# Odd experts' weighted sum moved from VectorE to ScalarE and GpSimd in a decoder layer's mixture of experts

## The reference

```python
logits = jnp.einsum('bsd,de->bse', input, Wg)
probs = jax.nn.softmax(logits, axis=-1)
top_vals, top_idx = jax.lax.top_k(probs, TOP_K)          # E = 8, TOP_K = 2
top_vals = top_vals / jnp.sum(top_vals, axis=-1, keepdims=True)
onehot = jax.nn.one_hot(top_idx, E, dtype=input.dtype)
mask = jnp.sum(onehot, axis=2)
scores = jnp.sum(onehot * top_vals[..., None], axis=2)
xm = input[None] * jnp.moveaxis(mask, -1, 0)[..., None]
h = jax.nn.relu(jnp.einsum('ebsd,edh->ebsh', xm, W1) + b1[:, None, None, :])
y = jnp.einsum('ebsh,ehd->ebsd', h, W2) + b2[:, None, None, :]
out = jnp.sum(y * jnp.moveaxis(scores, -1, 0)[..., None], axis=0)
```

## Time and profile before

| What | Value |
|---|---|
| Runs (median of three) | 512.89 us |
| Profiled execution, first to last instruction (its span) | 510.6 us |
| Mean granted TensorE clock | 0.843 |
| TensorE matmuls busy | 401.5 us (79%) |
| VectorE busy | 323.2 us (63%) |
| ScalarE busy | 159.2 us (31%) |
| GpSimd busy | 39.3 us (8%) |
| VectorE weighted adds, L1410 | 128 instructions, 36.0 us |

### The profile page before, as it was taken

How to read it: one execution, slowest core, us unless ns; L and a number is a source line. 1 busy time by engine, 2 the same in 40 slices (tenths; PEclk the granted TensorE clock), 3 DMA queues, 4 the chain that set the end, 5 groups by cost and what they waited for, 6 DMA issues and landing times.

```text
span 510.6 us, 8321 instructions
## 1 busy us (share of the span) xinstructions
PE 401.5 (79%) x2952; PEld 293.4 (57%) x2952; DVE 323.2 (63%) x1050; ACT 159.2 (31%) x267; POOL 39.3 (8%) x77
## 2 busy tenths in 40 slices
PE   1979999788973699984245689897998979887992
PEld 0647677467962699971023355565656546564672
DVE  2043464677999823368763576676897588777635
ACT  1252523512345211142021124422433244413430
POOL 7000000002980000000000000000000000000000
PEclk9989999997997555575555969999899989999997
DMA  7460201039653900000000000000020000000000
GB/s 246 105 186 1 42 0 22 1 75 296 166 145 88 119 3 3 3 2 0 1 1 27 15 21 1 0 22 0 2 62 2 21 0 21 0 0 1 22 2 21
DMA packets 48305, 22.23 MB, mean 44 GB/s; under 512 B 17768, under 2 KB 47632, under 8 KB 48016
## 3 DMA queue, kind: packets, MB, share of 16 engines
q1 hardware_dynamic: 31760, 13.40, 10.9%
q10 hardware_dynamic: 16512, 8.39, 6.0%
HBM read 18.64 MB, written 3.15 MB: 43 GB/s over the span
## 4 chain that ended last, share of the span: by engine, by line
PE 49%; DVE 31%; issue 9%; DMA 5%; ACT 3%; SPq 2%; DVEq 0%; ACTq 0%; POOL 0%
PE bank L460 9%; PE bank L493 5%; PE bank L691 5%; PE bank L699 5%; PE bank L721 5%; PE bank L733 4%; PE bank L442 4%; DVE prod L1430 3%; DVE inv L1432 3%; DVE as_t L1410 2%; DVE as_t L1232 2%; DVE nt L1143 2%; DVE nt L1142 2%; DVE as_t L1223 2%; DVE sm L1144 2%
## 5 line engine op out<-in xcount | busy, mean ns | idle before, releaser
L699 PEld LDWEIGHTS bank<-w_sb,as_t 128*128 128x128 f32 x512 | 61.0, 194 | 23.0 <-issue 18.8
L699 PE MATMUL bank<-w_sb,as_t 128*128 128x128 f32 x512 | 63.9, 280 | 5.0 <-ACT as_t L1002 5.0
L1002 ACT ACTIVATE as_t<-bank,cb 128x512 f32<-128x512 f32 x64 | 43.4, 687 | 76.0 <-PE bank L691 60.8
L691 PE MATMUL bank<-as_t,w_sb 128*128 128x512 f32 x128 | 66.5, 648 | 0.0
L1410 DVE SCALAR_TENSOR_TENSOR as_t<-bank,as_t 128x128 f32<-128x128 f32 x128 | 36.0, 344 | 23.4 <-PE bank L699 21.1
L460 PE MATMUL bank<-wtap,xc_pad 128*128 128x384 f32 x128 | 47.0, 514 | 3.8 <-DVE wtap L1157 3.8
L721 PE MATMUL bank<-vb,early 32*32 32x32 f32 x512 | 29.9, 236 | 11.7 <-DMA early<-inverses 11.7
L442 PE MATMUL bank<-ident,as_t 128*128 128x128 f32 (+1 forms) x64 | 12.1, 319 | 33.8 <-DVE as_t L1232 15.7
L1201 DVE TENSOR_TENSOR as_t<-bank,masks 128x512 f32 (+1 forms) x32 | 21.3, 690 | 26.7 <-PE bank L493 26.7
L460 PEld LDWEIGHTS bank<-wtap,xc_pad 128*128 128x128 f32 x128 | 25.0, 202 | 20.3 <-issue 4.3
L721 PEld LDWEIGHTS bank<-vb,early 32*32 32x32 f32 x512 | 28.2, 151 | 13.1 <-issue 12.3
(11 more groups left out here) (221 smaller groups left out, 647.5 us busy)
## 6 DMA issues: line engine op xcount, KB each, us to landing
toep<-taps_long ACTq DMA_DIRECT2D x8, 1024.0 KB, 7.0
toep<-x SPq DMA_DIRECT2D x8, 256.0 KB, 2.8
early<-x SPq DMA_DIRECT2D x4, 256.0 KB, 4.6
w_sb<-w SPq DMA_DIRECT2D x1, 1024.0 KB
w_sb<-w SPq DMA_DIRECT2D x2, 512.0 KB
blocks<-as_t SPq DMA_DIRECT2D x16, 64.0 KB, 2.0
early<-blocks SPq DMA_DIRECT2D x1, 1024.0 KB, 4.9
toep<-ctx_in SPq DMA_DIRECT2D x4, 256.0 KB, 3.4
```

What stands on the lines that cost most here:

```text
L691: pe.matmul(ps[4 + half][:, :], w1_sb[:, e, half * 128:half * 128 + 128], x2_c.rearrange("p b t -> p (b t)"), start=True, stop=True).then_ ...
L699: last = pe.matmul(bank(6 + e % 2)[:, b, :], hid[:, e % 2, half, b * L:(b + 1) * L], w2_sb[:, e, half, :], start=(half == 0), stop=(half = ...
L1002: act.activation(hid[:, e % 2, half, :], ps[4 + half][:, :], ACT.Relu, bias=c_of("b1", 2 * e + half)).then_inc(s["hid_ready"], 1)
```

## The change

The even experts' results (bank 6) are still summed on VectorE into acc. The odd experts' results (bank 7) are taken out of PSUM by ScalarE, which multiplies each sequence's 128 columns by its score (four activations of 128 x 128): expert 1 straight into a new tile `acc_odd`, experts 3, 5 and 7 into two alternating tiles `y_odd`. GpSimd adds these three to `acc_odd`, one 128 x 512 tensor_tensor each. `finish` on VectorE first adds `acc_odd` to acc. Each bank has its own counter: `y_added` now counts even experts and `y_scaled` odd ones. In all, VectorE loses 64 of its 128 weighted adds and gains 4 additions of 128 x 512, ScalarE gains 64 activations and GpSimd 12 additions.

```diff
--- before.py
+++ after.py
@@ -201,6 +201,8 @@
         hid = over(2 * 2 * N).rearrange("p (s k n) -> p s k n", s=2, k=2)
         acc = over3(G, D)
         fin = over3(G, D)
+        acc_odd = over3(G, D)
+        y_odd = over(2 * G * D).rearrange("p (k b c) -> p k b c", k=2, b=G)
         ps = [stack.enter_context(nc.psum_tensor(f"bank{i}", [128, 512], F32)) for i in range(8)]
@@ -242,7 +244,7 @@
                  "att_ps x2_ready "
                  "x2t_ps x2c_ready route_ps rmax_ready rexp_ready score_ready scoret_ps scoret_ready binit_ps hid_ps "
-                 "hid_ready y_ps sum_started y_added fin_ready").split()
+                 "hid_ready y_ps sum_started y_added y_scaled odd_added fin_ready").split()
         s = {n: sem(n) for n in names}
@@ -250,10 +252,10 @@
         CREDITS = {
             "pe": {"proj_ready": 1, "q_ps": 1, "kh_ps": 1, "kb_ps": 1, "gram_ps": 1,
                    "z_ps": 1, "st_ps": 1, "st2_ps": 1, "y_ps": 2},
-            "act": {"kb_c": 2, "proj_free": 2, "onc_ready": 1, "hid_ready": 2},
-            "dve": {"vb_ready": 1, "gram_kept": H, "x1_ready": 1, "x2_ready": 1, "ostats_ready": 1, "y_added": 2,
+            "act": {"kb_c": 2, "proj_free": 2, "onc_ready": 1, "hid_ready": 2, "y_scaled": 1},
+            "dve": {"vb_ready": 1, "gram_kept": H, "x1_ready": 1, "x2_ready": 1, "ostats_ready": 1, "y_added": 1,
                     "fin_ready": 1, "sum_started": 1},
-            "pool": {"v_kept": 1},
+            "pool": {"v_kept": 1, "odd_added": 1},
         }
         credit = {n: k for of in CREDITS.values() for n, k in of.items()}
@@ -429,8 +431,21 @@
             pool.wait_ge(s["stats_ready"], 4)
             stats_of(0)
             pool.wait_ge(s["stats_ready"], 5)
-            with pool.Fori(1, NG) as g:
-                stats_of(g)
+            stats_of(1)
+
+            def add_odd(g):
+
+                for e in (3, 5, 7):
+                    pool.wait_ge(s["y_scaled"], (E // 2) * g + e // 2 + 1 + credit["y_scaled"])
+                    pool.wait_ge(s["odd_added"], (E // 2 - 1) * g + e // 2 - 1 + credit["odd_added"])
+                    pool.tensor_tensor(out=acc_odd, in0=acc_odd, in1=y_odd[:, e // 2 % 2, :, :], op=ALU.add
+                                       ).then_inc(s["odd_added"], 1)
+
+            stats_of(2)
+            add_odd(0)
+            stats_of(3)
+            for g in range(1, NG):
+                add_odd(g)
         @block.tensor
@@ -693,7 +708,8 @@
             def result(g, e):
                 pe.wait_ge(s["hid_ready"], g * 2 * E + 2 * e + 2 + credit["hid_ready"])
-                pe.wait_ge(s["y_added"], g * E + e - 1 + credit["y_added"])
+                emptied = "y_scaled" if e % 2 else "y_added"
+                pe.wait_ge(s[emptied], g * (E // 2) + e // 2 + credit[emptied])
                 for b in range(G):
                     for half in range(2):
                         last = pe.matmul(bank(6 + e % 2)[:, b, :], hid[:, e % 2, half, b * L:(b + 1) * L],
@@ -1003,6 +1019,19 @@
                                    bias=c_of("b1", 2 * e + half)).then_inc(s["hid_ready"], 1)
+            def scaled(g, e):
+
+                act.wait_ge(s["y_ps"], g * E + e + 1 + credit["y_ps"])
+                if e == 1:
+                    act.wait_ge(s["score_ready"], g + 1)
+                    act.wait_ge(s["fin_ready"], g + credit["fin_ready"])
+                else:
+                    act.wait_ge(s["odd_added"], (E // 2 - 1) * g + e // 2 - 2 + credit["odd_added"])
+                to = acc_odd if e == 1 else y_odd[:, e // 2 % 2, :, :]
+                for b in range(G):
+                    last = act.activation(to[:, b, :], bank(7)[:, b, :], ACT.Copy, scale=score[:, b, e:e + 1])
+                last.then_inc(s["y_scaled"], 1)
+
             act.wait_ge(s["v_kept"], NG + credit["v_kept"])
             act.wait_ge(s["k_ready"], NG)
             act.activation(sq_g[:, :, :], src[:, :, 3, :], ACT.Square).then_inc(s["ssq_ready"], 1)
@@ -1081,11 +1110,15 @@
                 p, q = g - 1, g - 2
                 x1_columns(p)
                 x_columns(g)
+                if experts_left:
+                    scaled(q, 5)
                 st_columns(g)
                 source_gate(g)
                 if experts_left:
                     hidden(q, 7)
                 source_exp(g)
+                if experts_left:
+                    scaled(q, 7)
                 x2_columns(p)
                 route_exp(p)
                 hidden(p, 0)
@@ -1095,11 +1128,13 @@
                 hidden(p, 2)
                 keep_values(g)
                 score_columns(p)
+                scaled(p, 1)
                 hidden(p, 3)
                 st2_columns(g)
                 output_gate(g)
                 output_tanh(g)
                 hidden(p, 4)
+                scaled(p, 3)
                 hidden(p, 5)
                 on_columns(g)
                 hidden(p, 6)
@@ -1109,18 +1144,24 @@
                 step(g, True)
             p, q = NG - 1, NG - 2
             x1_columns(p)
+            scaled(q, 5)
             hidden(q, 7)
+            scaled(q, 7)
             x2_columns(p)
             route_exp(p)
             hidden(p, 0)
             hidden(p, 1)
             hidden(p, 2)
             score_columns(p)
+            scaled(p, 1)
             hidden(p, 3)
             hidden(p, 4)
+            scaled(p, 3)
             hidden(p, 5)
             hidden(p, 6)
+            scaled(p, 5)
             hidden(p, 7)
+            scaled(p, 7)
         @block.vector
@@ -1411,9 +1452,12 @@
                                                     scalar=score[:, b, e:e + 1], in1=acc[:, b, :],
                                                     op0=ALU.mult, op1=ALU.add)
                 last.then_inc(s["y_added"], 1)
-                dve.wait_ge(s["y_added"], g * E + e + 1 + credit["y_added"])
+                dve.wait_ge(s["y_added"], g * (E // 2) + e // 2 + 1 + credit["y_added"])
             def finish(g):
+                dve.wait_ge(s["odd_added"], (E // 2 - 1) * (g + 1) + credit["odd_added"])
+                dve.wait_ge(s["y_scaled"], (E // 2) * (g + 1) + credit["y_scaled"])
+                own(dve.tensor_tensor(out=acc, in0=acc, in1=acc_odd, op=ALU.add))
                 dve.wait_ge(stored, 16 * (g + 1))
                 layernorm(acc, fin, "fin_ready")
@@ -1484,16 +1528,12 @@
                 p, q = g - 1, g - 2
-                if experts_left:
-                    add(q, 5)
                 rotate_queries(p)
                 decay_scores(p)
                 source_logits(g)
                 if experts_left:
                     add(q, 6)
                 x2_norm(p)
-                if experts_left:
-                    add(q, 7)
                 source_weights(g)
                 route_max(p)
                 mixture(g)
@@ -1503,16 +1543,14 @@
                 mixture_stats(g)
                 start_sum(p)
                 add(p, 0)
-                add(p, 1)
                 rotate_keys(g)
                 add(p, 2)
                 gated(g)
-                add(p, 3)
                 x1_norm(g)
                 add(p, 4)
             step(1, False)
-            MIX_STEPS = 101
+            MIX_STEPS = 102
             start = base[1]
             with dve.Fori(2, NG) as g:
                 base[0], base[1] = start + (g - 2) * MIX_STEPS, 0
@@ -1520,24 +1558,18 @@
             assert base[1] == MIX_STEPS, base[1]
             base[0], base[1] = 0, start + (NG - 2) * MIX_STEPS
             p, q = NG - 1, NG - 2
-            add(q, 5)
             rotate_queries(p)
             decay_scores(p)
             add(q, 6)
             x2_norm(p)
-            add(q, 7)
             route_max(p)
             choose(p)
             finish(q)
             start_sum(p)
             add(p, 0)
-            add(p, 1)
             add(p, 2)
-            add(p, 3)
             add(p, 4)
-            add(p, 5)
             add(p, 6)
-            add(p, 7)
             finish(p)
```

## The result

Four runs of the changed kernel gave 526.05 to 528.07 us, median 526.49, against 512.76 (512.59 to 513.82) for the kernel before on the same chip: a ratio of 1.0275, 95% interval 1.0249 to 1.0302. The forecast was 519.0, its range 514.2 to 521.0: the sign was right, and the loss is more than twice the size forecast. The profiled spans are 525.2 and 510.6 us, 14.6 apart. Here and in the table of the experiments a median and a range take in all runs, and a ratio leaves out those over 1.5% above the fastest of their kernel.

A forecast was written before the change was run, and what follows sets the result against it. No single bound: a gapless VectorE stretch, a chain through three engines to `x1_norm`, and TensorE's tail. Blocking +3.0, `finish` less expert 7 +1.1 and the end +2.0 gave 512.89 + 6.1 = 519.0 us, range 514.2 to 521.0.

The forecast's parts named there:

- Blocking: In `gated`, GpSimd's addition for expert 3 holds the SBUF port against VectorE: 1.0 us in three steps, +3.0.
- The end: After the last result, the odd sum passes ScalarE, GpSimd and VectorE before the layernorm: 3.2 us, +2.0.
- `finish`, less expert 7's add: Steps 2 and 3: `finish`'s new addition, less what expert 7's removed add gains, costs 0.55 us each, +1.1.
- my 0.26: Gain at `route_max` from expert 7's removed add, left after GpSimd's blocking: start near 415.15 instead of 415.41.
- my 0.8: Cost in us of the new 128 x 512 addition in `finish`, in VectorE's gapless stretch of steps 2 and 3.
- Experts 1, 3 and 5: Removing these experts' adds from VectorE gains 0, since the tanh or TensorE is late next.
- The scalings, hidden: ScalarE's four scalings per expert, 1.15 us, fit ahead of its next needed work with 0.5 to 0.7 to spare.
- the sum itself: Blocking, `finish` less expert 7, and the end add up to +6.1 us on the span, giving 519.0 us.
- Rival 1: Nobody blocks anybody in the chain; only `finish` and the end cost: +2.6, 515.5 us; chance 27%.
- rival 2: VectorE is the bound where its adds stand in the chain, so experts 7 and 1 gain: -2.0, 510.9 us; 8%.
- rival 3: ScalarE becomes the bound, four scalings taking 2.4 us and delaying its column copies: +8.4, 521.3 us; 7%.
- rival 4: The end is longer by 1.0, nothing lost in the middle, within 0.2 to 1.0 us of before: 513.5; 8%.

The follow-up runs named there:

- e16: e2 with GpSimd's addition for expert 3 held until `gated` of the same step is done; median 519.95 us, ratio 1.0132.
- e2: Changed kernel with VectorE's steps 2 and 3 written out one after the other, without the loop; median 515.86 us, ratio 1.0073.
- e13: Kernel before plus ScalarE's 64 scalings, reading a constant SBUF tile and writing a buffer nobody reads; median 513.15 us, ratio 0.9986.
- e1: Changed kernel with 16 extra semaphore increments at the start of VectorE's program; median 524.03 us, ratio 1.0213.
- e14: Changed kernel with 40 extra semaphore increments at the start of VectorE's program; median 519.42 us, ratio 1.0103.
- e3: Kernel before with 104 extra semaphore increments at the start of VectorE's program; median 525.69 us, ratio 1.0200.
- e4: Changed kernel with GpSimd's addition for expert 3 held until `gated` of the same step is done; median 530.83 us, ratio 1.0347.
- e6: Changed kernel with all eight results of the last group added on VectorE as before; median 525.08 us, ratio 1.0243.
- e7p: e1 with expert 3's GpSimd addition held until `gated` is done and the last group added on VectorE; median 519.85 us, ratio 1.0119.
- e8: e1 with GpSimd's addition for expert 3 held until `gated` is done; median 523.14 us, ratio 1.0159.
- e9: e1 with the addition in `finish` cut to 8 columns; median 519.20 us, ratio 1.0106.

## Why the prediction was wrong

- **Blocking, 3.0 forecast.** Right: L1383 or L1385 pays 0.96 to 1.05 us in each step, and e16 takes it away. That it was L1383 and not L1385 that waited (in after) changed nothing.
- **The end, 2.0 forecast.** Right: 2.07.
- **`finish`, less expert 7's add, 1.1 forecast.** Too much: the stretch from `rotate_queries` to `start_sum` in step 3 changed by -0.06 in e2, whose step 3 begins at the same time as before's. GpSimd's addition for expert 7 blocks L1342 (L1301 before) as forecast, and `route_max` (L1420) comes 0.41 us earlier (415.00 for 415.41), for my 0.26. The new addition in `finish` costs 0.71, near my 0.8. What I hadn't reckoned with is the sources' weighted sum behind `route_max`, which ran 0.35 closer together, so that 0.76 was won ahead of `finish`; why it did isn't shown. Experts 1, 3 and 5: no gain, as forecast. Timeline of e2:

```profile
412.61 1.10 DVE L1342 TENSOR_TENSOR as_t<-as_t 128x16 f32<-128x16 f32 x1
...
415.00 0.19 DVE L1420 TENSOR_REDUCE as_t<-bank 128x4 f32<-128x32 f32 x1
```

- **The scalings, hidden.** Right (e13).
- So the forecast's own terms are worth 2.40 - 0.06 + 2.07 = 4.4 us in e2's profile, for 6.1. With 0.07 ahead of the first `gated`, 0.1 in the other stretches, and one stretch at 1.2 GHz fewer (-1.67), that is e2's +2.9.
- **The step that failed is the sum itself**: it held that all work that the change doesn't name takes the time it took. It had no term for two things. First, the diff makes VectorE's program 11 instructions shorter ahead of its loop, the loop then spans a block of code more, and the branch from step 2 back to step 3 waits 3.4 us for instructions (e1, e14 and e2 take it away, e3 brings it into the kernel before). Second, TensorE, idle behind that, comes back at half speed: 4.2 us more until `start_sum`, as in e3, which has the wait and none of the change. Together 7.7 us, more than all the forecast terms. So the 14.6 us of the profile are 2.9 of blocking, 2.1 at the end, 7.7 of stall and slow clock behind it, 1.6 ahead of the first `gated` (noise, see the table), and 0.4 elsewhere, put down to the clock (+0.9 in `wo` of step 1, +1.0 until `gated` of step 2, -1.5 in the tail).
- Rival 1 (515.5) fails on the blocking, rival 2 on every stretch, rival 3 on e13, rival 4 on the end and the blocking. None had the missing terms. The rows of the kernel before could not show them, since it has 0.79 us idle at that place and no transfer of instructions; counting VectorE's instructions ahead of and in the loop would have given the branch a chance of its own.

## What to carry to other kernels

An edit also moves the code behind it: where an engine's loop is about as long as the blocks of code that it holds, count its instructions before and after, give "the branch back now misses" a chance of its own, and test it with a few harmless instructions ahead of the loop or by writing the loop out. A wait put into TensorE's chain can cost twice its length through the granted clock (3.4 us and 4.2 behind it), so kernels are compared stretch by stretch between the same instructions, not by one median. An addition moved to an engine that shares a port with the first comes back as waiting wherever the two meet in the chain, and an instruction of 16 columns waits as long as one of 512.

## What the runs showed that I had not expected

- VectorE's missed branch: 3.4 us once (402.29 and 407.35 above), with five 8 KB transfers more than without, from a loop that begins 11 instructions earlier.
- The port is held for a whole GpSimd addition (1.27 us) against a VectorE instruction of 16 columns: 1.15 for 0.18. In the solve both were long.
- Behind the stall TensorE stayed at 1.2 GHz for 7 us, while the short drops that every kernel has lasted about 3; in e3, e4, e6, e7p, e8, e9 and e14 some lasted 10 to 14. Runs of one and the same variant spread over 3 to 11 us, where the kernel before mostly stays within 3. Only one run of each has a profile, so that the clock makes most of that spread is argued, not shown.
